# Four transformer blocks in one kernel: a length chain moved, row tests and a masked context on GpSimd, V biases folded, one norm on ScalarE and GpSimd

## The chip, the cores and the metric

The kernel runs on one core of one Trainium2 chip. The metric is the device time of one execution in microseconds (us), the lower the better. Five engines work side by side, each through its own instruction list in order, and wait for each other by semaphores: TensorE (PE), VectorE (DVE), ScalarE (ACT), GpSimd (POOL), and SyncE (SP), which only issues DMAs here.

## What is computed

32 batches of x and ctx, each 128 x 256 float32, go through four blocks with six attentions and two feed-forwards. Numbers 0 to 5 are the attentions, D = 256, 16 heads.

```python
# block L0 (attentions 0 and 1, heads of 16, no output weight)
mask0 = 1 - all(x == 0);  z = mha(x, x, Wq1, Wk1, Wv1, mask0, causal)     # attention 0
x1 = norm(x + z);         mask1 = 1 - all(x1 == 0)
z = mha(x1, ctx, Wq2, Wk2, Wv2, mask1)                                    # attention 1
x2 = norm(x1 + z)
z = (relu(x2 @ fc1.T + b1) * mask0 @ fc2.T + b2) * mask0;  x = norm(x2 + z)   # ("ff", 1)
# in mha: Q, K, V = (x|kv) @ W * mask;  energy = Q K^T
#         lengths = sum(energy[:, :, 0, :] != 0);  columns >= lengths become -inf;  softmax; @ V; * mask
# block L1: attention 2 (self, mask by row table), attention 3 (over ctx, mask by batch), then
#           gelu feed-forward 256 -> 1024 -> 256 ("ff", 3); biases on Q, K, V, output
# block L2: attention 4, heads of 64 over ctx ("wide"); block L3: attention 5 over ctx
# each attention: x = norm(x + softmax(Q K^T / sqrt(dk)) V @ Wo + bo)
```

## The kernel before

The 32 batches are worked in 4 rounds of 8 (LANES). In a round attention 0 is done for its 8 batches, then attention 1, and so on. One attention of one batch is a slot, n = 0 to 191; att(n) is its attention and batch(n) its batch. "Stage a" below is the eight slots of attention a.

`make_orders` (L125) writes each engine's order by hand: every item gets a time in slots, n plus an offset from the table NARROW or BROAD (L115 to L121), and each engine's list is sorted by it. The items of up to five slots are so interleaved. `tile(at, reader, ...)` puts an item on PE at `at` and its copy out of PSUM on `reader` at `at + AFTER_PE` (0.03). With the offsets of a narrow slot, seen from slot n's start:

- XT: transpose of X (ACT copies it out). K, Q, V: the three products, K and Q a slot early. ACT copies K; Q with a scale in four pieces into Qx (two halves of the heads), and waits for nothing else than PE. `keys`: GpSimd makes Kx of K in four operations. V goes to V16 by ACT (attentions 0, 1) or by DVE with the bias row added (2, 3, 5).
- S and T: scores of one unit (8 heads), row by row and turned. A slot has two units, u = 2n and 2n+1. One score step `ST` on PE does S of one unit and T of an earlier one in two PSUM tensors SC0 and SC1: at 0.0 S of 2n and T of 2n-3, at 0.5 S of 2n+1 and T of 2n-2. `free_scores` has PE wait until the former user of the bank is read: for an S before, until its maximum is taken; for a T before, until its exp is done. So the S of 2n+1 waits for the exp of 2n-3.
- `max` (DVE, L1084): row maxima of S, at 0.12 and 0.62. `MT` (0.86): PE turns them, DVE adds them to Qx, and the turned scores then hold score minus maximum. `exp` (ACT, L862 to L871): at 0.12 and 0.62, in a slot after.
- PV: probabilities by V, copied to OT by ACT; E1: transpose back, DVE divides by the sum; E2, E3: transpose and output weight (attentions 2, 3, 5). Attentions 0 and 1 have no output weight, and GpSimd adds the residual.
- `L` (attentions 0 and 1): the energies of row 0. GpSimd lays out q0, PE makes the product (L at n-0.42), and DVE goes through a chain: not equal, count, reciprocal, factor, row of -BIG behind the length, and two additions into Kx (seven instructions, L1046 to L1063). The S of the slot waits for it.
- `norm`: bn_stats, bn_aggr, plus eps, centre times gamma on DVE (LN); the power -0.5 on GpSimd (rstd, L1234); times rstd plus beta on DVE (LN end, L1166).
- Row tests: `seen0`, `seen1`: DVE takes the largest absolute value of each row and compares it with 0. The mask of attention 1's keys: GpSimd makes a diagonal of seen1 (`token mask`), PE multiplies ones by it (`SM`, L625), DVE multiplies the turned context CT by the result (L1015).
- Feed-forward: XF transposes X, F1 with ACT's relu or gelu, F2, DVE adds X, then a norm ("ff"). Offsets above 3 and 4 put E1 to F2 three to five slots later, so the small feed-forward (of attention 1) falls into the last four slots of stage 1 and the first four of stage 2, the large one into stage 3's last four and the wide stage.

PE's results go through four PSUM tiles in turn (M0 to M3, `free_tile`): a tile is written again when the item four back is copied out.

```python
                if before[0] == "S":
                    pe.wait_ge(maxima, done("max", before[1]))
                else:
                    pe.wait_ge(probs, done("exp", before[1]))
```

The weights, biases and rows are loaded once at the start; x, ctx and masks of later batches by SP in time.

Of the kernel before, what the change touches and what calls it, by code (L numbers as in the profile page):

```python
# [122 lines left out]


def make_orders():  # L125
# [10 lines left out]
    def norm(at, what, n):  # L136
        put("DVE", at, "LN", what, n)
        put("POOL", at + 0.01, "rstd", what, n)
        put("DVE", at + LN_END, "LN end", what, n)

    steps = {}
    for n in range(SLOTS):
# [32 lines left out]
        tile(n + o["V"], "ACT" if a in (0, 1) else "DVE", "V", n, 0)  # L175
# [62 lines left out]
def score_bank_users():  # L238
# [1076 lines left out]
```

## Time and profile before

| what | value |
|---|---|
| median of 3 runs | 2756.04 us (2753.0 to 2758.52) |
| the profiled execution | 2755.75 us, its span 2753.6 us |
| mean granted clock of TensorE | 0.952 |
| PE busy | 2519.1 us, 91% |
| DVE, ACT, POOL busy | 1600.2 (58%), 1376.2 (50%), 827.1 (30%) us |
| idle of POOL before the power of the norm | 1202.6 us in 256 |
| chain that ended last | PE 72%, DVE 11%, issue 7%, POOL 5%, ACT 4% |

The span is the time from the first to the last instruction. Busy times are of the engine's own instructions; idle time of an engine that isn't the bottleneck costs nothing. The granted clock is the share of TensorE's full 2.4 GHz; its other level is 1.2 GHz. PEld rows are weight loads, which lie beside the products.

### The profile page before, as it was taken

How to read it: one execution, taken by the hardware profiler on the slowest of the kernel's cores; microseconds unless marked ns; L12 is line 12 of the kernel's file. 1: busy time of each engine (PE TensorE's matmuls, PEld its weight loads, DVE VectorE, ACT ScalarE, POOL GpSimd, SP SyncE). 2: the span in 40 equal slices, each digit the busy share in tenths (PEclk: the TensorE clock that was granted, in tenths of full speed). 3: DMA queues.
4: the chain of work that ended last, by engine and by line, in shares of the span. 5: the costliest groups of instructions: out<-in, count | busy, mean ns of one | idle time of the engine just before them, and what ended most of it. 6: DMA issues, size and time to landing. Idle time of an engine off the chain costs nothing.

```text
span 2753.6 us, 70667 instructions
## 1 busy us (share of the span) xinstructions
PE 2519.1 (91%) x28737; PEld 2094.6 (76%) x28737; DVE 1600.2 (58%) x3528; ACT 1376.2 (50%) x3364; POOL 827.1 (30%) x1412
## 2 busy tenths in 40 slices
PE   6879999999887999999988899999998889999998
PEld 5667887887766788787766688888786668888876
DVE  4677753445766775344576676544466676644446
ACT  2344565554444456555544456555454445655544
POOL 1234322223233432222323343222232344312222
PEclk8889999999998999999999899999999889999999
DMA  7000000000100000000000000000000000000000
GB/s 245 7 2 2 2 2 1 1 1 10 36 6 2 2 2 2 1 1 2 21 26 4 2 2 2 2 1 1 1 27 23 2 2 2 2 1 1 1 1 17
DMA packets 23778, 32.28 MB, mean 12 GB/s; under 512 B 2305, under 2 KB 22177, under 8 KB 23329
## 3 DMA queue, kind: packets, MB, share of 16 engines
q1 hardware_dynamic: 23456, 27.78, 3.1%
q8 instruction: 229, 3.75, 0.6%
q14 instruction: 93, 0.75, 0.1%
HBM read 23.57 MB, written 4.19 MB: 10 GB/s over the span
## 4 chain that ended last, share of the span: by engine, by line
PE 72%; DVE 11%; issue 7%; POOL 5%; ACT 4%; POOLq 0%; DMA 0%; DVEq 0%; SPq 0%; ACTq 0%
PE M L522 40%; PE SC L685 12%; PE M L528 7%; PE M L721 4%; DVE nmax L1084 3%; POOL Kx L1202 3%; PE M L738 2%; PE SC L584 2%; PE SC L703 2%; PE SC L559 2%; ACT Pr L862 2%; DVE Kx L1063 1%; POOL Y L1228 1%; DVE stats L1151 1%; DVE len_row L1057 1%
## 5 line engine op out<-in xcount | busy, mean ns | idle before, releaser
L1234 POOL TENSOR_TENSOR rstd<-rstd,half 128x1 f32<-128x1 f32 x256 | 184.5, 721 | 1202.6 <-DVE rstd L1155 1201.7
L522 PE MATMUL M<-XT,W 128*128 128x128 f32 x4096 | 540.8, 287 | 2.5 <-ACT H L904 1.5
L522 PEld LDWEIGHTS M<-XT,W 128*128 128x128 f32 x4096 | 519.0, 203 | 20.0 <-issue 2.7
L1084 DVE TENSOR_REDUCE nmax<-SC 128x8 f32<-128x1024 f32 x320 | 389.6, 1217 | 92.0 <-PE SC L685 92.0
L1202 POOL TENSOR_SCALAR Kx<-K,own,k_ones 128x128 f32<-128x128 f32 x640 | 279.6, 451 | 498.7 <-ACT K L815 357.1
L685 PEld LDWEIGHTS SC<-Kx,Qx 32*128 32x128 f32 x5120 | 341.6, 200 | 91.9 <-issue 87.7
L685 PE MATMUL SC<-Qx,Kx 32*128 32x128 f32 x5120 | 398.4, 297 | 0.9 <-DVE Qx L1023 0.9
L685 PE MATMUL SC<-Kx,Qx 32*128 32x128 f32 x5120 | 394.7, 296 | 1.5 <-DVE nmax L1084 1.5
L685 PEld LDWEIGHTS SC<-Qx,Kx 32*128 32x128 f32 x5120 | 333.8, 198 | 3.3 <-issue 1.3
L871 ACT ACTIVATE Pr<-SC 128x1024 f32<-128x1024 f32 x256 | 261.6, 1022 | 69.7 <-PE SC L584 44.3
L841 ACT ACTIVATE Qx<-M,q_bias,q_scale 128x128 f32<-128x128 f32 x640 | 241.8, 474 | 23.4 <-PE M L522 23.4
L862 ACT ACTIVATE Pr<-SC,nmax_w 128x128 f32<-128x128 f32 x512 | 139.0, 383 | 183.3 <-DVE nmax_w L1087 158.1
L1128 DVE TENSOR_TENSOR Y<-M,X 128x256 f32<-128x256 f32 x128 | 54.1, 423 | 271.2 <-PE M L522 271.2
L522 PE MATMUL M<-CT,W 128*128 128x128 f32 x1536 | 207.5, 286 | 0.0
L522 PEld LDWEIGHTS M<-CT,W 128*128 128x128 f32 x1536 | 189.0, 197 | 14.7 <-issue 7.6
L815 ACT ACTIVATE K<-M 128x256 f32<-128x256 f32 x64 | 24.5, 383 | 336.5 <-PE M L522 336.5
L522 PE MATMUL M<-W,CT 128*128 128x512 f32 (+1 forms) x512 | 191.6, 497 | 0.0
L818 ACT ACTIVATE K<-M,CB 128x128 f32<-128x128 f32 x192 | 60.2, 366 | 260.8 <-PE M L522 260.8
L721 PE MATMUL M<-Pr,V 128*32 128x128 f32 x5120 | 173.8, 277 | 0.0
L1252 POOL TENSOR_TENSOR Pr<-Pr,wrec 128x1024 f32<-128x1024 f32 x64 | 121.3, 1895 | 156.7 <-DVE wrec L1099 156.7
L528 PE MATMUL M<-ident,nmax 128*128 128x128 f32 x160 | 48.4, 302 | 130.0 <-DVE nmax L1084 129.9
L798 ACT ACTIVATE XT<-M 128x256 f32<-128x256 f32 x256 | 97.8, 390 | 137.3 <-PE M L528 137.2
(127 smaller groups left out, 4460.3 us busy)
## 6 DMA issues: line engine op xcount, KB each, us to landing
X<-x SPq DMA_DIRECT2D x32, 128.0 KB, 2.1
c_in<-ctx_in SPq DMA_DIRECT2D x32, 128.0 KB, 2.1
out<-X SPq DMA_DIRECT2D x32, 128.0 KB, 1.7
RV<-row_vec SPq DMA_DIRECT2D x1, 2304.0 KB, 12.1
W<-w_k SPq DMA_DIRECT2D x5, 256.0 KB, 9.0
W<-w_q SPq DMA_DIRECT2D x5, 256.0 KB, 12.1
W<-w_v SPq DMA_DIRECT2D x5, 256.0 KB, 7.8
W<-w_f SPq DMA_DIRECT2D x1, 1024.0 KB, 8.9
```

The costliest lines, as they stand in the source:

```text
L522: last = pe.matmul(dst, a, b, start=(k == 0), stop=(k == len(lhsTs) - 1))
L528: last = pe.transpose(dst[:, i * P:(i + 1) * P], src[:, i * P:(i + 1) * P], ident[:, :])
L685: filled[at] = pe.matmul(dst, lhsT, rhs, start=(starting and i == 0), stop=(i == len(line) - 1), skip_group_check=True)
L721: last = pe.matmul(tile_of(it)[32 * t:32 * t + 32, b * P:(b + 1) * P], on_ring(V16, "narrow", n)[:, 4 * b + t, :], p[:, at:at + P], start= ...
L798: act.activation(XT[i % len(XT)][:, :], tile_of(it)[:, 0:D], ACT.Copy).then_inc(tile_act, 1)
L841: last = act.activation(q[:, half_of, c * P:(c + 1) * P], tile_of(it)[:, c * P:(c + 1) * P], ACT.Identity, bias=q_bias[:, which, c, half_o ...
L862: last = act.activation(p[:, i * P:(i + 1) * P], SC[u % 2][:, i * P:(i + 1) * P], ACT.Exp, bias=nm[:, i:i + 1])
L871: last = act.activation(p[:, :], SC[u % 2][:, :], ACT.Exp)
L1084: dve.tensor_reduce(nm, SC[h][:, :].rearrange("p (g c t) -> p g c t", c=KC, t=P), AX_X, ALU.max, negate=True).then_inc(maxima, 1)
L1202: last = pool.tensor_scalar(kx[:, half_of, c * P:(c + 1) * P], k[:, c * P:(c + 1) * P], own[:, half_of:half_of + 1], k_ones[:, half_of, c: ...
L1234: pool.tensor_tensor(r[:, :], r[:, :], half[:, :], ALU.pow).then_inc(rstd_done, 1)
L1252: pool.tensor_tensor(p, p, on_ring(wrec, "wide", u)[:, :].unsqueeze(2).to_broadcast([P, HU, P]), ALU.mult).then_inc(wide_norm, 1)
```

## The change

It changes offsets of the order, moves work between engines and folds constants.

- Order: on PE, L goes from n-0.42 (0.58 in a slot, behind the second score step) to n-0.64 (0.36, ahead of it). `AFTER_SCORES`, the distance of maxima and exps from their score steps, goes from 0.12 to 0.19. PV, MT, XT, K, Q, XF, F1, F2, LN get new offsets. The context's transpose goes from stage 0 to two slots ahead of its slot of attention 1.
- q0 is made from a copy of Q's first row's column by ACT (`q_col`), ahead of the four copies of Q; GpSimd does one operation on 8 columns for each half, as before.
- The length chain has six instructions in place of seven: the comparison gives -1/BIG in place of 1, the reciprocal of the count then is the value itself.
- `seen0`, `seen1`: the comparison with 0 goes to GpSimd, the largest value stays on DVE.
- The mask of attention 1: GpSimd multiplies the context itself by seen1 after PE has turned it once (`context`), PE turns it again (`CM`, two transposes), ACT copies that to CmT. Token mask, SM and DVE's product go.
- The V biases of attentions 2 to 5 no longer are added to V or to the context. Since probabilities sum to one they are multiplied by the output weight once (items VT and VB in the slots 9 to 12) and added to the rows o2 to o5. V of attention 2 is copied by ACT. The wide context is one copy in place of four with a bias.
- The norm of ("ff", 1): ACT does scale and shift (`normalise`), GpSimd multiplies by gamma and adds beta (`affine`), in place of two operations on DVE. The shift is one more small operation on GpSimd.
- Y has two buffers, mv two, absmax four.

```diff
-NARROW = dict(XT=-1.20, SM=-1.25, K=-0.92, Q=-0.86, L=-0.42, V=0.30, CT=0.40, MT=0.86, PV=2.66, E1=3.20, E2=3.54,
-              E3=3.74, XF=4.40, F1=4.62, F2={1: 4.90, 3: 5.10},
-              seen0=-1.15, keys=-0.88, q0=-0.78, mask_row=-0.30, residual=3.30, LN=3.40, SF=0.14)
+NARROW = dict(XT=-1.14, CM=-1.10, CT=-1.92, K=-0.94, Q=-0.88, L=-0.64, V=0.28, MT=0.93, PV=2.62, E1=3.20, E2=3.54,
+              E3=3.72, XF=4.24, F1=4.40, F2={1: 4.66, 3: 4.95}, seen0=-1.0, context=-1.75, keys=-0.80, q0=-0.86,
+              mask_row=-0.30, residual=3.32, LN=3.84)
+V_BIAS_AT = {2: 9.32, 3: 10.32, 4: 11.32, 5: 12.32}
-AFTER_PE, AFTER_SCORES = 0.03, 0.12
-LN_END = 0.25
+AFTER_PE, AFTER_SCORES = 0.03, 0.19
+LN_END = 0.22
+def by_pool(norm):
+    return norm[0] == "ff" and att(norm[1]) == 1
...
     def norm(at, what, n):
         put("DVE", at, "LN", what, n)
         put("POOL", at + 0.01, "rstd", what, n)
-        put("DVE", at + LN_END, "LN end", what, n)
+        if by_pool((what, n)):
+            put("ACT", at + 0.12, "normalise", what, n)
+            put("POOL", at + 0.18, "affine", what, n)
+        else:
+            put("DVE", at + LN_END, "LN end", what, n)
...
-            put("DVE", n + o["seen0"], "seen0", b)
+            put("DVE", n + o["seen0"], "largest0", b)
+            put("POOL", n + o["seen0"] + 0.08, "seen0", b)
+        if a == 1:
             tile(n + o["CT"], "ACT", "CT", b)
-        if a == 1:
-            put("POOL", n + o["SM"] - 0.20, "token mask", n)
-            tile(n + o["SM"], "DVE", "SM", n)
+            put("POOL", n + o["context"], "context", b)
+            tile(n + o["CM"], "ACT", "CM", b)
...
-        tile(n + o["V"], "ACT" if a in (0, 1) else "DVE", "V", n, 0)
+        tile(n + o["V"], "ACT" if a in (0, 1, 2) else "DVE", "V", n, 0)
...
-        put("SP", slot(b, 0) - 1.5 if b >= 2 else -9, "c", b)
+        put("SP", slot(b, 1) - 3 if b >= 2 else -9, "c", b)
...
-                    sp.wait_ge(tile_full, done("tile", ("CT", b - 2)))
+                    sp.wait_ge(tile_full, done("tile", ("CM", b - 2)))
...
+                elif kind == "CM":
+                    b = it[1]
+                    pe.wait_ge(cm_done, done("batch", b))
+                    turn(tile_of(it), c_in[b % 2], KC).then_inc(tile_full, 1)
+                elif kind == "VB":
+                    a = it[1]
+                    if a == WIDE:
+                        pe.wait_ge(v_bias_wide, 1)
+                        by_tokens(it, "o4", split(Qw, 4) + split(Kw, 4), D)
+                    else:
+                        evicted(("VT", a))
+                        by_tokens(it, f"o{a}", split(Qw, KC), D)
...
+                elif kind == "normalise":
+                    key = it[1:]
+                    i = AT["affine"][key]
+                    act.wait_ge(mean_done, i + 1)
...
+                    act.activation(xn[i % 2], on_ring(Y, "norm", key)[:, :], ACT.Identity, bias=shift[i % 2][:, 0:1],
+                                   scale=rstd[j][:, 0:1]).then_inc(normalised, 1)
...
+                        act.activation(q_col[i % 2][:, :], chunks(tile_of(it)[:, 0:D])[:, :, 0], ACT.Copy,
+                                       scale=DK ** -0.5).then_inc(q_first, 1)
...
-                    dve.reciprocal(crec[:, :], cnt[:, :]).then_inc(len_rec, 1)
-                    dve.wait_ge(len_rec, done("length", n))
-                    dve.scalar_tensor_tensor(out=lval[:, :], in0=crec[:, :], scalar=-BIG, in1=cnt[:, :], op0=ALU.mult,
-                                             op1=ALU.mult).then_inc(len_val, 1)
+                    dve.reciprocal(lval[:, :], cnt[:, :]).then_inc(len_val, 1)
...
+                    pool.tensor_scalar(c_in[b % 2][:, :], c_in[b % 2][:, :], seen1[lane(b)][:, 0:1], None,
+                                       ALU.mult).then_inc(cm_done, 1)
...
+                        pool.tensor_scalar(shift[i % 2][:, :], mv[AT["norm"][key] % 2][:, 0:1], r[:, 0:1], -1.0, ALU.mult,
+                                           ALU.mult).then_inc(mean_done, 1)
+                elif kind == "affine":
...
+                    pool.tensor_tensor(xn[i % 2], xn[i % 2], row(name + "g"), ALU.mult).then_inc(affine_half, 1)
+                    pool.wait_ge(affine_half, i + 1)
+                    pool.tensor_tensor(X[lane(b)][:, :], xn[i % 2], row(name + "b"), ALU.add).then_inc(normed_pool, 1)
```

## Rows read from the trace of the kernel before

**Rows 1.** The page: the span, and busy time of each engine.

```profile
span 2753.6 us, 70667 instructions
PE 2519.1 (91%) x28737; PEld 2094.6 (76%) x28737; DVE 1600.2 (58%) x3528; ACT 1376.2 (50%) x3364; POOL 827.1 (30%) x1412
```

**Rows 2.** Stretches of attentions 0 to 5: length, PE, PEld, DVE, ACT, POOL, PEclk, DMA.

```profile
713.30:813.00 99.70, 83.79 (x1101) 65.55 (x1100) 67.13 (x171) 41.59 (x89) 28.71 (x66) 0.93 0.05 16
813.00:919.30 106.30, 86.77 (x1092) 73.18 (x1093) 74.57 (x177) 45.09 (x98) 42.45 (x83) 0.86 0.01 2
919.30:1001.70 82.40, 82.40 (x1146) 65.65 (x1148) 57.52 (x124) 42.76 (x95) 32.41 (x59) 1.00 0.01 2
1001.70:1098.60 96.90, 96.02 (x1196) 84.27 (x1189) 58.16 (x131) 59.94 (x129) 26.93 (x47) 1.00 0.01 2
1098.60:1314.30 215.70, 204.89 (x1654) 172.16 (x1652) 91.55 (x170) 114.93 (x348) 52.90 (x51) 0.98 0.01 1
1314.30:1389.30 75.00, 71.10 (x1012) 59.31 (x1012) 49.58 (x106) 39.05 (x84) 23.38 (x48) 0.98 0.08 25
```

**Rows 3.** Waits: who for whom; us in all, times, longest us.

```profile
PE M L528 <- DVE nmax L1084: 129.9, 71, 3.5
...
PE M L625 <- POOL seen_diag L1219: 30.0, 32, 1.5
...
PE M L738 <- ACT Pr L878: 16.4, 12, 2.1
```

**Rows 4.** Timeline, PE, stage 2: start us, length us, instructions.

```profile
974.17 1.95 PE L522 MATMUL M<-XT,W 128*128 128x128 f32 x16
...
977.26 0.59 PE L559 MATMUL SC<-mask_ss_b,ident_b 128*128 128x512 bf16 x2
...
979.34 0.38 PE L528 MATMUL M<-ident,O 128*128 128x128 f32 x2
...
979.65 1.08 PE L721 MATMUL M<-Pr,V 128*32 128x128 f32 x32
...
981.95 0.59 PE L559 MATMUL SC<-mask_ss_b,ident_b 128*128 128x512 bf16 x2
```

**Rows 5.** Timeline, ACT, the same slot.

```profile
975.27 0.62 ACT L818 ACTIVATE K<-M,CB 128x128 f32<-128x128 f32 x2 [2.69 <-PE M L522]
...
975.78 1.02 ACT L871 ACTIVATE Pr<-SC 128x1024 f32<-128x1024 f32 x1
...
976.68 1.51 ACT L841 ACTIVATE Qx<-M,q_bias,q_scale 128x128 f32<-128x128 f32 x4
...
980.94 0.61 ACT L885 ACTIVATE OT<-M 128x512 f32<-128x512 f32 x1
```

**Rows 6.** Timeline, PE, a slot of stage 0; in brackets the idle time before.

```profile
773.14 0.44 PE L528 MATMUL M<-ident,X 128*128 128x128 f32 x2
775.94 0.39 PE L528 MATMUL M<-ident,nmax 128*128 128x128 f32 x1 [2.35 <-DVE nmax L1084]
```

**Rows 7.** Timeline, DVE, a feed-forward slot of stage 1.

```profile
870.75 0.47 DVE L1137 SCALAR_TENSOR_TENSOR Y<-M,seen,X 128x256 f32<-128x256 f32 x1
...
871.25 0.43 DVE L1151 BATCH_NORM_STATS2 stats<-Y 128x6 f32<-128x256 f32 x1
...
871.92 0.15 DVE L1155 TENSOR_SCALAR rstd<-mv 128x1 f32<-128x1 f32 x1
...
872.39 1.22 DVE L1084 TENSOR_REDUCE nmax<-SC 128x8 f32<-128x1024 f32 x1
```

**Rows 8.** Groups by line and form: busy us, mean ns; idle before, releaser.

```profile
L1234 POOL TENSOR_TENSOR rstd<-rstd,half 128x1 f32<-128x1 f32 x256 | 184.5, 721 | 1202.6 <-DVE rstd L1155 1201.7
...
L1245 POOL TENSOR_TENSOR X<-X,RV 128x256 f32<-128x256 f32 x160 | 117.0, 736 | 22.2 <-PE M L528 22.1
...
L798 ACT ACTIVATE XT<-M 128x256 f32<-128x256 f32 x256 | 97.8, 390 | 137.3 <-PE M L528 137.2
...
L522 PE MATMUL M<-W,OT 128*128 128x256 f32 x512 | 116.2, 380 | 0.7 <-ACT OT L889 0.7
```

More of the change, by code:

```diff
@@ L197, in make_orders @@
         if a == 0:
-            put("DVE", n + o["LN"] + LN_END + 0.01, "seen1", b)
+            put("DVE", n + o["LN"] + LN_END + 0.02, "largest1", b)
+            put("POOL", n + o["LN"] + LN_END + 0.08, "seen1", b)
         if a in XT_FOR_FF:
@@ L208, in make_orders @@
         put("PE", at, "ST", parts.get("S"), parts.get("T"))
+    for a, at in V_BIAS_AT.items():
+        if a == WIDE:
+            put("DVE", at, "v bias wide", a)
+        else:
+            tile(at, "DVE", "VT", a)
+        tile(at + 0.40, "DVE", "VB", a)
     for b in range(BATCH):
@@ L271 @@
     "norm_end": [it[1:] for it in pick("DVE", {"LN end"})],
+    "affine": [it[1:] for it in pick("POOL", {"affine"})],
     "add": [it[1:] for it in pick("POOL", {"add"})],
@@ L279 @@
 BANK_BEFORE = score_bank_users()
-assert INDEX["norm"] == INDEX["rstd"] == INDEX["norm_end"] and INDEX["length"] == INDEX["q0"]
+assert INDEX["norm"] == INDEX["rstd"] and INDEX["norm_end"] == [key for key in INDEX["norm"] if not by_pool(key)]
+assert INDEX["affine"] == [it[1:] for it in pick("ACT", {"normalise"})] and INDEX["length"] == INDEX["q0"]
 assert INDEX["narrow"] == INDEX["keys"] == INDEX["e1"]
@@ L389, in build @@
             sem("len_done"))
+        v_bias_wide = sem("v_bias_wide")
         recip_done, summed = sem("recip_done"), sem("summed")
@@ L486, in _ @@
                 elif kind == "store":
-                    sp.wait_ge(normed, done("norm", ("att", slot(b, 5))))
+                    sp.wait_ge(normed, done("norm_end", ("att", slot(b, 5))))
                     sp.dma_start(out[b, :, :], X[lane(b)][:, :]).then_inc(stored[lane(b)], 16)
@@ L613, in _ @@
                         what, a = XT_AFTER[j]
-                        pe.wait_ge(normed, done("norm", (what, slot(b, a))))
+                        if by_pool((what, slot(b, a))):
+                            pe.wait_ge(normed_pool, done("affine", (what, slot(b, a))))
+                        else:
+                            pe.wait_ge(normed, done("norm_end", (what, slot(b, a))))
                     turn(tile_of(it), X[lane(b)], KC).then_inc(tile_full, 1)
@@ L883, in _ @@
                         act.wait_ge(tile_full, done("tile", ("E1", before[1]) if before[0] == "PV" else ("E3", before[1] // 2)))
-                    if kind == "PV":
-                        last = act.activation(o[:, :], tile_of(it)[:, :], ACT.Copy)
-                    else:
-                        for t in range(4):
-                            last = act.activation(o[:, t * P:(t + 1) * P], tile_of(it)[:, t * P:(t + 1) * P],
-                                                  ACT.Identity, bias=bias("v4", 4 * (it[1] % 2) + t))
-                    last.then_inc(tile_act, 1)
+                    act.activation(o[:, :], tile_of(it)[:, :], ACT.Copy).then_inc(tile_act, 1)
                 elif kind == "E2":
@@ L900, in _ @@
                     a, i = att(n), AT["ff"][n]
+                    if a == 3:
+                        once(normed_pool, LANES * (batch(n) // LANES + 1))
                     if i:
@@ L967, in _, with free_sum @@
             dve.wait_ge(masks_turned, 1)
+            dve.tensor_scalar(iota[:, :], iota[:, :], -1.0 / BIG, None, ALU.mult)
             dve.tensor_copy(key_bias[:, :], M[TILES - 1][:, 0:BATCH]).then_inc(ready_dve, 1)
+            def free_sum(key):
+                i = AT["norm"][key]
+                if i >= len(Y):
+                    before = INDEX["norm"][i - len(Y)]
+                    if by_pool(before):
+                        once(normalised, done("affine", before))
+                    else:
+                        once(centred, done("norm_end", before))
             for it in ORDER["DVE"]:
@@ L1125, in _ @@
                     dve.wait_ge(added, done("add", (XT_FOR_ATT[att(n)], batch(n))))
-                    if AT["norm"][("att", n)]:
-                        once(centred, AT["norm"][("att", n)])
+                    free_sum(("att", n))
                     dve.tensor_tensor(on_ring(Y, "norm", ("att", n))[:, :], tile_of(it)[:, 0:D],
@@ L1133, in _ @@
                     dve.wait_ge(added, done("add", (XT_FOR_FF[a], b)))
-                    once(centred, AT["norm"][("ff", n)])
+                    free_sum(("ff", n))
                     y = on_ring(Y, "norm", ("ff", n))
@@ L1226, in _ @@
                     if i >= len(Y):
-                        pool.wait_ge(centred, i - len(Y) + 1)
+                        before = INDEX["norm"][i - len(Y)]
+                        if by_pool(before):
+                            pool.wait_ge(normalised, done("affine", before))
+                        else:
+                            pool.wait_ge(centred, done("norm_end", before))
                     pool.tensor_tensor(on_ring(Y, "norm", key)[:, :], on_ring(O, "e1", n)[:, :], X[lane(b)][:, :],
@@ L1239, in _ @@
                     once(rows_in if name == "g0" else rows_late_in, 16)
+                    if name[0] == "o":
+                        once(tile_dve, done("tile_dve", ("VB", int(name[1]))))
                     if name == "g0":
```

153 lines of the change are left out of this document (95 added, 58 removed).

## The prediction, made before the changed kernel was run

> **What bounds the kernel now.** First the page's busy line: PE 2519.1 of 2753.6 us (91%), no other engine above 58% [rows 1]. Then the table of stretches over one of the four rounds (8 batches, 48 slots, 676 us): 99.7 us for the eight slots of attention 0, 106.3 for attention 1, then 82.4, 96.9, 215.7 (the wide one) and 75.0 [rows 2]. In stages 2 and 3 PE is busy without a hole and its granted clock is 1.00, the level of 2.4 GHz. In stages 0 and 1 it is busy for 84 and 87 us only, and the clock is 0.93 and 0.86, so part of the time passes at 1.2 GHz. The waits say why: PE's transpose of the row maxima (MT) waits 129.9 us in all for `nmax` on DVE, and the token-mask product 30.0 us for `seen_diag` [rows 3]. In a slot of stage 0 the first is one hole of 2.35 us behind the transpose of X [rows 6]: on DVE the second maximum stands behind the length chain. So stages 2, 3 and most of 5 are bound by PE's own stream and can only lose by a new wait; stages 0 and 1 are bound by waits and can win.
>
> **ScalarE's order is turned round.** A slot has two score steps, ST0 and ST1. ST1 writes into the bank in which ST0's turned scores stand, so (free_scores) it waits for their exp; the next slot's ST0 waits in the same way for the exp of ST1's. With AFTER_SCORES at 0.19 for 0.12, Q at n+0.15 and K at n+0.09, the first exp, so far between K and Q, stands behind Q. PV goes from 0.69 to 0.65, so the second exp (0.62, now 0.69) stands behind the context copy. ScalarE takes its queue in order: an exp whose scores are ready still waits for the product ahead of it. That ACT is idle half of the span does not help, since it idles while PE makes Q.
> Price in stage 2. K and Q run on PE from 974.17 to 976.12, ST1 starts 977.26, PV 979.65, the next ST0 981.95 [rows 4]. ACT has exp from 975.78 (1.02), then Q (four in 1.51) [rows 5]. After: Q 976.15 to 977.66, exp right behind with 0.1 of overlap to 978.58, ST1 at 978.61, which is 1.35 later. PV then ends on PE at 979.65 + 1.35 + 1.08 = 982.08, its copy (0.61 [rows 5]) at 982.72, the second exp at 983.64; the next ST0, due at 983.30, starts 983.67, 0.37 more. Together 1.72 a slot. It holds where PE has only E1 and V between Q and ST1: the last four slots of stage 2, the first four of stage 3, the last five of stage 5, 13 x 1.72 = 22.4. The slot before these in stage 5 has less on PE and loses some 2.7 by the same walk.
> In four slots of stage 3 the product F1 now stands ahead of ST1 and needs the copy of XT, which stands behind the exp. With K's start as 0: Q's copies end 3.5, exp 4.42, XT's copy 4.75, F1 starts 4.8 where PE is free at 3.4: 1.4 x 4 = 5.6.
>
> **Eight slots with the small feed-forward (four of stage 1, four of stage 2).** F2 now stands at 0.66 on PE and its sum at 0.69 on DVE, put ahead of the second maximum (also 0.69); `normalise` stands on ACT at 0.83, ahead of XT, CM and the next K, and nothing on ACT passes it. Walk in stage 2: F1 starts 4.8 as above (1.4 late), ST1 5.7, PV 7.8, F2 8.7 to 9.7; on DVE the sum 0.47 and the maximum 1.22, to 11.36 [rows 7]; only then MT (1.4 late), ST0, and K at 13.6. The other branch from the maximum: bn_stats to eps 0.82, with the hand-over 0.91 [rows 7], the power on GpSimd 0.72 [rows 8], the shift (128x1, not in this trace; between 0 and that power's 0.72, I take 0.2 since it has no power), normalise and XT's copy 0.39 each [rows 8]: K at 13.95. Before: a later slot is 974.17 to 981.95 plus the 2.08 of a score step [rows 4], 9.86, which leaves 82.4 - 39.4 = 43.0 for the first four. After 55.7 (four of 13.95, less one shorter ST, plus one E2): +12.7. In stage 1 CM and CT come on top and one slot has no length chain: 14.0, 14.0, 13.6, 13.1 = 54.7.
>
> **Where the length chain goes.** In the other slots of stages 0 and 1 L stands on PE ahead of ST1, and on DVE between the maxima, so MT's 2.35 us go. (q0 is now made from a first copy of two columns of Q; it costs ACT between 0 and the 0.38 of a whole 128 columns, I take 0.25, as it has hardly anything to read.) What is late next is again the exp. Stage 0: Q on PE ends 1.95, ACT is through at 4.6, ST1 at 4.63, PV ends 3.16 later, its copy and the exp 4.72 later, ST0 at 9.38, K at 11.46: 8 x 11.46 = 91.7 at the full clock, with two waits of 1.1 and 1.35 in place of the one. Stage 1, first four: CT moves Q's end to 2.18, ST1 4.85, ST0 8.6, K 9.65; with 1.1 for two longer score steps 39.7, and with the last four 94.4. Before, the clock cost these stages (1 - 0.93) x 99.7 = 7.0 and (1 - 0.86) x 106.3 = 14.9 [rows 2]. Waits stay in every slot, so I put 5.3 and 9 back, and 3 in the first half of stage 2; the bounds are 0 and the costs of before.
>
> **The other parts.** CM's two transposes (0.38, as E2's two in rows 4) take the place of the mask product inside the walks above. DVE loses the product with the mask, two passes of one norm, V's row sum and one link of the chain; PE waits for DVE in the places of [rows 3] alone, so elsewhere this is worth nothing. GpSimd gains `context` (256 columns: up to the 0.74 of its two-input sum) and the affine, 2 x 0.74 [rows 8]; it is idle 70% [rows 1], and the affine ends 1.1 us after the next K starts, before `keys` has its input. PVW as one copy in place of four: PE waited 16.4 us in all for the copies beside it [rows 3], so 0 to -4.1 a round, I take -2. Folding the V biases once in round 0: the wide one as an E3 of the wide attention, 116.2/32 = 3.6 us [rows 8], three narrow ones a quarter of it each, 2.7, and three turned rows 1.1, all on PE: 7 us once. SP reloads c_in behind CM, three slots ahead of its use, some 30 us: hidden.
>
> **Sum of a round.** Stage 0: 97.0 - 99.7 = -2.7. Stage 1: 94.4 + 9 - 106.3 = -2.9. Stage 2: 12.7 + 3 + 6.9 = +22.6. Stage 3: 6.9 + 5.6 = +12.5. Stage 4: -2. Stage 5: 5 x 1.6 (its ST is shorter) + 2.7 = +10.7. That is +38.2, 153 in four rounds, 160 with the 7: on the profiled execution's own 2755.75 (its span and 2.15 around it), which is 0.3 below the median 2756.04, 2916 us.
>
> **Rivals.**
> A. The clock spreads. Waits of 1.3 us now stand in stages 2, 3 and 5. For: the stages with a wait in every slot are those at 0.93 and 0.86. Against: that was one of 2.35. If the 254 us of these stages fall to 0.93 they lose 18 more a round: 2916 + 72 = 2988. The Trainium skill ("TensorE: Matmul & The Clock Gate", section "A second HAM failure mode: psum-queue depth-cycling") says that frequent short idling between groups of matmuls makes the clock swing between its two levels; no row here shows whether waits of 1.3 us do.
> B. Faster: VectorE's relief is worth all it can be. The waits for maxima and mask (160 us [rows 3]) and the clock of stages 0 and 1 (4 x 21.9 = 88) come back whole, because DVE and not ACT sets the pace there: 2756 - 248 + 7 + 170 (the losses of stages 2, 3 and 5 at full clock) = 2685. It is faster than before once over 177 of the 248 are won. For: the largest wait on the page is its target. Against: in the walk the exp ends later than the maximum in each of these slots.
> C. F2, maximum and normalise overlap more than in my walk, and no clock is lost: 2916 - 4 x 17.3 - 4 x 7 (half of what those slots lose or fail to win) = 2819.
> D. Gains and losses cancel within 0.2%, about what a measurement here can tell from nothing.
>
> **Numbers.** Forecast 0.64, A 0.12, B 0.11, C 0.10, D 0.03. The forecast's own range is 2847 (no clock lost, 20.9 x 4 + 7) to 2960; with most of A and C it is 2825 to 2990. Faster 0.11, same 0.03, slower 0.86.
>
> **What would show it.** In the changed trace PE waits at the score steps for ACT Pr, about 1.3 us in most narrow slots and over 100 us in all; the wait for nmax is gone from stage 0 and stands in the eight feed-forward slots, about 1.4 each; stage 2 is near 105 us and stage 5 near 86. I am wrong if PE shows no waits for the exp, or if stages 2, 3 and 5 keep 82.4, 96.9 and 75.0.

## The result, and the profile after

The changed kernel takes 2831.39 us (median of 4 runs, 2828.23 to 2832.09) where the one before takes 2757.28 (2753.0 to 2758.53): 1.0269 times, 95% interval 1.0252 to 1.0287. The direction is the forecast's and the size is half of it: 76 us between the profiled executions (2832.09 against 2755.75), where 160 were forecast. The time lies below the forecast's own range (2847 to 2960). The late slots along ScalarE's queue came out as the walks had them; what was put too high was the cost of TensorE's clock and the time of the wide stage.

The page after, beside [rows 1]: PE is busy 40 us less and the span is 77 us longer.

```profile
span 2830.2 us, 70971 instructions
PE 2479.0 (88%) x28803; PEld 2033.3 (72%) x28803; DVE 1547.6 (55%) x3282; ACT 1384.2 (49%) x3332; POOL 926.0 (33%) x1572
```

The same round by stretches, in the columns of [rows 2] (length, PE, PEld, DVE, ACT, POOL, PEclk, DMA share, GB/s):

```profile
715.00:807.00 92.00, 79.31 (x1101) 59.85 (x1101) 68.47 (x156) 41.39 (x95) 33.39 (x75) 1.00 0.06 17
807.00:906.00 99.00, 79.43 (x1098) 68.22 (x1099) 66.41 (x143) 48.59 (x116) 48.55 (x92) 0.93 0.03 9
906.00:1012.30 106.30, 86.28 (x1129) 64.61 (x1128) 50.83 (x114) 49.32 (x111) 44.84 (x79) 1.00 0.01 2
1012.30:1124.20 111.90, 100.80 (x1284) 86.73 (x1284) 60.22 (x136) 62.88 (x130) 29.72 (x52) 1.00 0.01 2
1124.20:1328.60 204.40, 199.26 (x1649) 167.64 (x1648) 93.91 (x176) 104.60 (x299) 50.42 (x47) 1.00 0.01 1
1328.60:1414.40 85.80, 72.87 (x937) 60.87 (x936) 44.80 (x87) 38.64 (x84) 24.49 (x48) 0.92 0.05 14
```

| stage of round 1 | before | forecast | after | clock before, after |
|---|---|---|---|---|
| 0 | 99.7 | 97.0 | 92.0 | 0.95, 1.00 |
| 1 | 106.3 | 103.4 | 99.0 | 0.84, 0.93 |
| 2 | 82.4 | 105.0 | 106.3 | 1.00, 1.00 |
| 3 | 96.9 | 109.4 | 111.9 | 1.00, 1.00 |
| 4 (wide) | 215.7 | 213.7 | 204.4 | 0.98, 1.00 |
| 5 | 75.0 | 85.7 | 85.8 | 0.95, 0.92 |
| sum | 676.0 | 714.2 | 699.4 | |

The clocks before are not those of [rows 2]. Its stretches start 9.8 us behind the first score step of each stage: the first step with the causal mask in this round starts at 703.52, where the rows begin at 713.30. The lengths hold to 0.1 us, but busy times and clocks are of the shifted stretches. In the right place stages 0, 1 and 5 read

```profile
703.50:803.10 99.60, 84.05 (x1111) 65.58 (x1110) 68.43 (x176) 42.45 (x91) 27.90 (x64) 0.95 0.07 20
803.10:909.50 106.40, 86.51 (x1081) 72.90 (x1081) 71.75 (x173) 43.69 (x93) 40.27 (x81) 0.84 0.01 2
1304.50:1379.50 75.00, 69.19 (x937) 58.26 (x936) 44.32 (x88) 39.41 (x89) 24.33 (x47) 0.95 0.07 20
```

The loss is in stages 2 and 3 (+38.9) and in stage 5 (+10.8); the other three gained 26.3. PE's waits after, whole span (who for whom; us in all, times, longest), against [rows 3]:

```profile
PE M L546 <- ACT XT L835: 70.4, 67, 1.6
PE SC L722 <- ACT Pr L929: 69.2, 92, 1.6
PE SC L583 <- ACT Pr L929: 68.8, 87, 1.2
PE M L552 <- DVE nmax L1143: 59.1, 52, 1.6
...
PE SC L722 <- ACT Pr L927: 14.4, 20, 1.3
PE M L546 <- ACT CmT L845: 12.4, 7, 1.8
```

The score steps wait for an exp (L927, L929) 152 us in all, and did not before. The wait for the maxima fell from 129.9 to 59.1, the one for the mask is gone, and a new one of 70.4 for ScalarE's copy of XT stands at K and F1. A late slot of stage 2 on PE shows the first two, beside [rows 4]:

```profile
979.46 1.95 PE L546 MATMUL M<-XT,W 128*128 128x128 f32 x16
...
981.68 1.03 PE L546 MATMUL M<-W,XT 128*128 128x256 f32 x4
983.91 0.60 PE L583 MATMUL SC<-mask_ss_b,ident_b 128*128 128x512 bf16 x2 [1.21 <-ACT Pr L929]
```

and ScalarE in the same slot, beside [rows 5]:

```profile
980.55 0.62 ACT L869 ACTIVATE K<-M,CB 128x128 f32<-128x128 f32 x2 [2.95 <-PE M L546]
981.44 1.50 ACT L899 ACTIVATE Qx<-M,q_bias,q_scale 128x128 f32<-128x128 f32 x4 [0.27 <-PE M L546]
982.83 1.03 ACT L929 ACTIVATE Pr<-SC 128x1024 f32<-128x1024 f32 x1
```

K is copied, then ScalarE goes straight on to Q, and the exp, whose scores had long been ready, begins only at 982.83. PE has nothing left at 982.70 and stands for 1.21 us. The late slots of stage 2 are 11.7 us long (9.9 before): +1.8, where the walk gave 1.72.

A slot with the small feed-forward, first on PE, then on DVE, GpSimd and ScalarE:

```profile
908.83 2.02 PE L546 MATMUL M<-XT,W 128*128 128x128 f32 x16 [1.13 <-ACT XT L835]
...
913.73 1.13 PE L546 MATMUL M<-XT,W 128*128 128x128 f32 x8 [1.35 <-ACT XT L835]
...
920.17 0.33 PE L552 MATMUL M<-ident,nmax 128*128 128x128 f32 x1 [1.49 <-DVE nmax L1143]
```
```profile
918.50 0.48 DVE L1195 SCALAR_TENSOR_TENSOR Y<-M,seen,X 128x256 f32<-128x256 f32 x1 [6.39 <-PE M L546]
918.90 1.22 DVE L1143 TENSOR_REDUCE nmax<-SC 128x8 f32<-128x1024 f32 x1
```
```profile
920.93 0.55 POOL L1314 TENSOR_TENSOR rstd<-rstd,half 128x1 f32<-128x1 f32 x1 [6.20 <-DVE rstd L1220]
921.58 0.53 POOL L1321 TENSOR_SCALAR shift<-mv,rstd 128x1 f32<-128x1 f32 x1
```
```profile
922.15 0.60 ACT L853 ACTIVATE H<-Y,shift,rstd 128x256 f32<-128x256 f32 x1 [3.17 <-POOL shift L1321]
922.66 0.36 ACT L835 ACTIVATE XT<-M 128x256 f32<-128x256 f32 x1
```

The second maximum starts 0.40 after the feed-forward's sum, which waited 6.39 us for F2, and ends at 920.12: MT waits 1.49 (forecast 1.4). ScalarE's queue stands 3.17 us at `normalise`; the copy of XT behind it needs nothing of it (PE had turned that X at 918.30, before `normalise` began). Such slots of stage 2 last 14.3, 14.9, 14.9 and 15.2 us; the walk gave 13.95. In stage 1 they last 12.6, 16.4, 15.9 and 13.8 (walk: 14.0, 14.0, 13.6, 13.1).

### The profile page after: what moved, and what is told of

It reads as the page before. It is cut to its first block, busy times and chain, and to the rows that moved or that the text cites. A ratio compares the mean times of both kernels' runs of the same rounds, so it can differ in the third digit from the quotient of the medians.

```text
span 2830.2 us, 70971 instructions
## 1 busy us (share of the span) xinstructions
PE 2479.0 (88%) x28803; PEld 2033.3 (72%) x28803; DVE 1547.6 (55%) x3282; ACT 1384.2 (49%) x3332; POOL 926.0 (33%) x1572
## 4 chain that ended last, share of the span: by engine, by line
PE 62%; ACT 14%; issue 12%; POOL 8%; DVE 3%; ACTq 0%; POOLq 0%; DMA 0%; SPq 0%; DVEq 0%
PE M L546 34%; PE SC L722 10%; ACT Pr L929 6%; PE M L552 5%; ACT Qx L899 4%; PE M L758 4%; PE M L775 2%; PE SC L740 2%; PE SC L608 2%; POOL Kx L1268 2%; PE SC L583 2%; ACT Pr L927 1%; POOL X L1343 1%; ACT Pr L920 1%; POOL H L1328 1%
## 5 line engine op out<-in xcount | busy, mean ns | idle before, releaser
L546 PE MATMUL M<-XT,W 128*128 128x128 f32 x4096 | 528.4, 281 | 70.4 <-ACT XT L835 70.4
L1314 POOL TENSOR_TENSOR rstd<-rstd,half 128x1 f32<-128x1 f32 x256 | 174.6, 682 | 1260.6 <-DVE rstd L1220 1260.6
L546 PEld LDWEIGHTS M<-XT,W 128*128 128x128 f32 x4096 | 499.0, 196 | 99.9 <-ACT XT L835 83.3
L722 PEld LDWEIGHTS SC<-Kx,Qx 32*128 32x128 f32 x5120 | 319.4, 188 | 141.9 <-ACT Pr L929 77.3
L722 PE MATMUL SC<-Kx,Qx 32*128 32x128 f32 x5120 | 369.1, 283 | 58.5 <-ACT Pr L929 57.6
L722 PE MATMUL SC<-Qx,Kx 32*128 32x128 f32 x5120 | 371.2, 283 | 0.9 <-DVE Qx L1089 0.9
L722 PEld LDWEIGHTS SC<-Qx,Kx 32*128 32x128 f32 x5120 | 310.3, 186 | 3.1 <-ACT Pr L929 1.1
L942 ACT ACTIVATE OT<-M 128x512 f32<-128x512 f32 x224 | 134.3, 599 | 315.6 <-PE M L758 215.7
L929 ACT ACTIVATE Pr<-SC 128x1024 f32<-128x1024 f32 x256 | 263.2, 1028 | 9.2 <-PE SC L722 7.2
L546 PEld LDWEIGHTS M<-CT,W 128*128 128x128 f32 x1536 | 187.6, 196 | 14.9 <-issue 6.7
L758 PEld LDWEIGHTS M<-Pr,V 128*32 128x32 f32 x5120 | 130.0, 109 | 33.2 <-issue 27.9
L546 PE MATMUL M<-W,H 128*128 128x256 f32 x640 | 152.0, 384 | 0.0
## 6 DMA issues: line engine op xcount, KB each, us to landing
W<-w_q SPq DMA_DIRECT2D x5, 256.0 KB, 12.4
```

Source lines behind the costliest of these rows:

```text
L546: last = pe.matmul(dst, a, b, start=(k == 0), stop=(k == len(lhsTs) - 1))
L722: filled[at] = pe.matmul(dst, lhsT, rhs, start=(starting and i == 0), stop=(i == len(line) - 1), skip_group_check=True)
L758: last = pe.matmul(tile_of(it)[32 * t:32 * t + 32, b * P:(b + 1) * P], on_ring(V16, "narrow", n)[:, 4 * b + t, :], p[:, at:at + P], start= ...
L929: last = act.activation(p[:, :], SC[u % 2][:, :], ACT.Exp)
L942: act.activation(o[:, :], tile_of(it)[:, :], ACT.Copy).then_inc(tile_act, 1)
L1314: pool.tensor_tensor(r[:, :], r[:, :], half[:, :], ALU.pow).then_inc(rstd_done, 1)
```

## The experiments

Theory T, in all of them: the loss is ScalarE's order, exps and maxima put behind work that waits for PE (AFTER_SCORES 0.19), with the wait at `normalise`; the length chain's new place is a gain on its own. Its rival R: the maxima on DVE, or the new operations themselves (context, affine, copies of CM), set the pace. Each kernel was timed beside the kernel before; ratios are to that, with the 95% interval.

**The exps alone back.**

```diff
-            put("ACT", n + T_STEP[h] + AFTER_SCORES, "exp", u)
+            put("ACT", n + T_STEP[h] + 0.12, "exp", u)
```

> The changed kernel with the exps alone put back to 0.12 and 0.62 (maxima stay at 0.19 and 0.69). Theory 1 (the exp behind Q and behind the context copy is what PE waits for in the score steps): the waits of PE at score steps for ACT Pr, 36.6 us a round in the changed kernel's trace, go; a slot of stage 0 falls from 11.5 to about 9.5, a late slot of stage 2 from 11.7 to 9.9, of stage 5 from 9.8 to 8.3; feed-forward slots keep their wait for the maximum. About 35 to 45 us a round less: 2831 -> 2650 to 2690. Rival (the exp only looks late because VectorE or the feed-forward chain sets the pace, and the wait moves on): less than 40 us in all, 2790 or more. Rival 2 (a tighter stream loses the full clock again): waits go but the mean clock falls below 0.96, 2720 to 2760.

Measured 2695.6 us, 0.9771 (0.9746 to 0.9796): 136 us less than the changed kernel, by one number, and 6 above the expected range. The waits of the score steps for the exp are gone, and stages 2 and 5 are 97.7 and 75.8.

**The maxima alone back.**

```diff
-            put("DVE", n + S_STEP[h] + AFTER_SCORES, "max", u)
+            put("DVE", n + S_STEP[h] + 0.12, "max", u)
```

> The changed kernel with the maxima alone put back to 0.12 and 0.62 (exps stay at 0.19 and 0.69), so the second maximum comes before F2's sum on VectorE. Theory 1: PE's waits at MT in the eight small feed-forward slots (14 us a round) go, but K still waits for normalise and XT behind it on ScalarE, so a slot falls from 14.9 to about 13.3: 10 to 13 us a round, 2831 -> 2780 to 2790. Rival (normalise sets the whole of these slots): the same within 10 us. Rival 2 (waits only add up): the full 14 and more, below 2775.

Measured 2792.31, 1.0128 (1.0111 to 1.0145): 39 us less, 2 above the expected range. It is stages 1 and 2, the slots with the feed-forward (99.0 to 92.6, 106.3 to 102.6), where the waits for nmax fall from 59.1 to 16.3 us in all; the exp waits stay. Maxima and exps are two separate costs of one number.

**Both back.**

```diff
-AFTER_PE, AFTER_SCORES = 0.03, 0.19
+AFTER_PE, AFTER_SCORES = 0.03, 0.12
```

> The changed kernel with AFTER_SCORES back at 0.12, all other parts of the change kept. Theory 1: both gains add, 2600 to 2650, well under the kernel before (2757), because the moved length chain is worth what it was meant for once the exp is in time. Rival (the change loses by its other parts, the norm on ScalarE and GpSimd and the extra transposes): 2757 or more.

Measured 2661.68, 0.9661 (0.9645 to 0.9677), a little above the expected range: the parts give 136 + 39 = 175, both together 170. So all the rest of the change makes the kernel 3.4% faster. ScalarE in a late slot of stage 2, to be held against the one above:

```profile
921.95 0.62 ACT L869 ACTIVATE K<-M,CB 128x128 f32<-128x128 f32 x2 [2.69 <-PE M L546]
922.46 1.02 ACT L929 ACTIVATE Pr<-SC 128x1024 f32<-128x1024 f32 x1
923.36 1.51 ACT L899 ACTIVATE Qx<-M,q_bias,q_scale 128x128 f32<-128x128 f32 x4
```

The exp fills the time in which ScalarE would have waited for Q. The largest wait that remains is 64.1 us for XT's copy, which stands behind `normalise`; the norm's own experiments are below.

**The late order in the kernel before.** The same number alone, on the other side.

```diff
-AFTER_PE, AFTER_SCORES = 0.03, 0.12
+AFTER_PE, AFTER_SCORES = 0.03, 0.19
```

> The kernel before with AFTER_SCORES 0.19 alone. Theory 1: 1.35 to 1.7 us in each narrow slot of stages 2, 3 and 5, and in stages 0 and 1 the later score step also moves the length chain: 40 to 58 us a round, 2920 to 2990. Rival (harmless by itself, only with K and Q earlier does it turn the order): Q stands at 0.17 in that kernel, so 0.19 turns it as well; if the time stays within 20 us of 2757 the exp is not what PE waits for.

Measured 3009.92, 1.0922 (1.0906 to 1.0939), again above the range: +252 here, against 170 in the changed kernel. Its waits and its stage 0 show why:

```profile
PE M L528 <- DVE nmax L1084: 179.0, 71, 3.5
PE SC L685 <- ACT Pr L871: 82.4, 91, 1.6
PE SC L559 <- ACT Pr L871: 72.6, 90, 1.4
PE SC L685 <- ACT Pr L869: 49.3, 44, 2.0
```
```profile
764.70:885.60 120.90, 92.06 (x1111) 70.32 (x1110) 70.36 (x179) 42.23 (x91) 27.87 (x64) 0.88 0.06 17
```

With the chain at its old place the late maximum lengthens MT's wait as well, 129.9 to 179.0 us, and the clock of stage 0 goes to 0.88. The waits for the exp are also longer here, 204.3 us in these three rows against 152.4 in the changed kernel. The cost of a late order depends on what it adds to.

**The chain's place, from both sides.** In the changed kernel, L alone back:

```diff
-NARROW = dict(XT=-1.14, CM=-1.10, CT=-1.92, K=-0.94, Q=-0.88, L=-0.64, ...
+NARROW = dict(XT=-1.14, CM=-1.10, CT=-1.92, K=-0.94, Q=-0.88, L=-0.42, ...
```

> The changed kernel with L alone back at n-0.42: behind the second score step on PE, ahead of the second maximum on VectorE. Theory (the move is worth the 2.35 us wait of MT in each slot with a length chain, and the clock that this long wait costs): stage 0 back above 100 us with its clock near 0.9, stage 1 above 105: 20 to 30 us a round more, 2831 -> 2910 to 2950. Rival (the exp sets these slots, so the place of L is worth nothing here): within 20 us of 2831. Of the clock: if the length of a single wait decides it, not their sum, the clock falls in stage 0 in this run, where PE has one wait of over 2 us again, and stays at 1.00 in stage 2, whose waits sum to 23 us in the changed kernel too.

Measured 2953.7, 1.0706 (1.0683 to 1.0729): 122 us more than the changed kernel and just above the expected range: without the chain's new place the change would have lost 195. MT waits again, 14.9 us in stage 0 and 15.3 in stage 1:

```profile
746.50:853.20 106.70, 82.83 (x1101) 62.40 (x1101) 63.97 (x152) 41.70 (x95) 32.76 (x74) 0.97 0.05 16
853.20:965.10 111.90, 82.84 (x1099) 70.36 (x1099) 61.53 (x147) 48.45 (x114) 49.34 (x93) 0.92 0.02 6
```

I had expected a clock near 0.9 in stage 0; it is 0.97. And in the kernel before, the offsets that belong to the chain's place (K, Q, L, `keys`, q0, the residual, LN and its end):

```diff
-NARROW = dict(XT=-1.20, SM=-1.25, K=-0.92, Q=-0.86, L=-0.42, ...
+NARROW = dict(XT=-1.20, SM=-1.25, K=-0.94, Q=-0.88, L=-0.64, ...
-              seen0=-1.15, keys=-0.88, q0=-0.78, mask_row=-0.30, residual=3.30, LN=3.40, SF=0.14)
+              seen0=-1.15, keys=-0.80, q0=-0.82, mask_row=-0.30, residual=3.32, LN=3.84, SF=0.14)
-LN_END = 0.25
+LN_END = 0.22
```

> The kernel before with the length chain's part of the order alone: K -0.94, Q -0.88, L -0.64, keys -0.80, q0 -0.82, residual 3.32, LN 3.84 and its end 0.22; AFTER_SCORES stays 0.12, nothing moves between engines. Theory 1 (the place of L ahead of the second maximum is what makes stages 0 and 1 fast, and no moved work is needed for it): MT's waits of 30 us a round mostly go, and the clock of stages 0 and 1 returns to over 0.97: 30 to 45 us a round, 2757 -> 2580 to 2640. Rival (without the early copy q_col the product L waits for Q's four copies, and without GpSimd's help VectorE is short): 2690 or more.

Measured 2656.67, 0.9642 (0.9627 to 0.9656): 100 us faster than before, by offsets alone, yet short of the expected 2580 to 2640. LN moved too (3.40 to 3.84) and was not tried by itself, so only the run above is of L alone. Its first waits suggest what the early copy of two columns of Q (q_col) is for:

```profile
PE M L522 <- POOL q L1189: 68.9, 62, 2.1
PE M L528 <- DVE nmax L1084: 51.7, 56, 1.6
```

Without that copy q0 comes from the last of Q's four copies, and the earlier L waits for it, about 1.1 us in 62 slots. In the changed kernel PE waits for q once, for 1.0 us. No run has q_col as its only difference.

**The norm on ScalarE and GpSimd, with the exps and maxima back.** First taken away (the eight normalisations a round go back to VectorE):

```diff
-    return norm[0] == "ff" and att(norm[1]) == 1
+    return False
...
-                    if a == 3:
-                        once(normed_pool, LANES * (batch(n) // LANES + 1))
```

> Built on e3 (AFTER_SCORES 0.12, the rest of the change kept): the norm of the small feed-forward goes back to VectorE whole, no normalise on ScalarE and no affine on GpSimd. Theory 1 (PE's waits of K and XT in the eight feed-forward slots, 7.3 us each in stages 1 and 2 of a round, come from normalise standing ahead of XT, CM and K on ScalarE): they go, 8 to 14 us a round, 2662 -> 2605 to 2630. Rival (VectorE is short in these slots, so its two operations come back as a wait for the maxima): 2650 or more, with the wait of MT for nmax up by as much.

Measured 2596.04, 0.941 (0.939 to 0.943): 66 us less than with it, more than expected; the waits for XT's copy fall from 64.1 to 22.8 us. Then kept, but later in the two queues:

```diff
-            put("ACT", at + 0.12, "normalise", what, n)
-            put("POOL", at + 0.18, "affine", what, n)
+            put("ACT", at + 0.30, "normalise", what, n)
+            put("POOL", at + 0.36, "affine", what, n)
```

> Built on e3: normalise stays on ScalarE and the affine on GpSimd, but both 0.18 of a slot later, behind XT and CM. Theory 1: as in e5 the waits of K go, and VectorE stays relieved: 2600 to 2625, at or below e5. Rival (what delays K is the time of the whole norm, or GpSimd, not the place in ScalarE's queue): as e3 within 10 us.

Measured 2605.11, 0.9446 (0.9423 to 0.9469): 57 of the 66 us come back by place alone; the 9 that are left are above the expected "at or below" the run with the norm on VectorE. The waits for XT's copy are 32.8 us here. So the work cost little, and its place ahead of XT, CM and K most. That it is the place in ScalarE's queue is what these waits say; GpSimd's part was moved in the same run, and the two were not separated.

**Four copies of the wide PV again, in the changed kernel.**

```diff
-                    act.activation(o[:, :], tile_of(it)[:, :], ACT.Copy).then_inc(tile_act, 1)
+                    if kind == "PV":
+                        last = act.activation(o[:, :], tile_of(it)[:, :], ACT.Copy)
+                    else:
+                        for t in range(4):
+                            last = act.activation(o[:, t * P:(t + 1) * P], tile_of(it)[:, t * P:(t + 1) * P], ACT.Copy)
+                    last.then_inc(tile_act, 1)
```

> The changed kernel with the wide context copied in four pieces again (without a bias, same output). The wide stage fell from 215.7 to 204.4 us where -2 was forecast. Theory 1 (the moved feed-forward and the clock made that, the one copy little): 0 to 4 us a round, 2831 -> 2831 to 2847. Rival (the single copy shortens the chain TP, PVW, E3 that PE waits for): 5 to 9 us a round, 2851 to 2867.

Measured 2826.51, 1.0251 (1.0223 to 1.0278), stage 4 still 204.4. The single copy is worth nothing: with four the time is 5 us lower, just outside the expected range, and the interval overlaps that of the changed kernel.

**The feed-forward's place, in the changed kernel.**

```diff
-              E3=3.72, XF=4.24, F1=4.40, F2={1: 4.66, 3: 4.95}, ...
+              E3=3.72, XF=4.40, F1=4.62, F2={1: 4.90, 3: 5.10}, ...
```

> The changed kernel with the feed-forward's offsets back (XF 4.40, F1 4.62, F2 4.90 and 5.10), so F1 stands behind the second score step and F2 behind MT. Asks where the unforeseen gain of the wide stage (215.7 -> 204.4) came from. Theory 1 (one F2 of 3.6 us falls in stage 3 instead of the wide stage, and the shorter waits keep its clock full): the wide stage returns to 209 to 216 us, stage 3 falls by 5 to 8 us (its F2 moves out, its waits of F1 for XT's copy go), the two together 4 to 6 less than the 316 of the changed kernel; the eight small feed-forward slots lose the MT wait and the F1 wait, 2 us each: 2831 -> 2740 to 2790 in all. Rival (the moved feed-forward is what made the wide stage short): stages 3 and 4 together rise, 2831 or more.

Measured 2794.21, 1.0136 (1.012 to 1.0151). The time came within the range and its parts did not all: stages 1 and 2 are 23 shorter, but stages 3 and 4 together rise from 316.3 to 328.4 where 4 to 6 less was expected.

```profile
987.20:1108.20 121.00, 101.81 (x1269) 88.06 (x1269) 60.72 (x135) 62.47 (x130) 29.09 (x52) 0.96 0.01 2
1108.20:1315.60 207.40, 203.52 (x1665) 171.37 (x1665) 94.52 (x178) 105.38 (x299) 49.86 (x47) 1.00 0.01 1
```

With F1 behind ST1 nothing stands between Q and that score step, and the wait for the late exp is in the open: the waits for L927 are 57.9 us in all here, against 14.4. In the changed kernel F1 covered them.

**A version out of this.** Exps and maxima back, the norm on VectorE, and F1 just behind ST1 (F1=4.53 for 4.40), so that it no longer waits for XT's copy:

> Built on e5 (AFTER_SCORES 0.12, norm on VectorE): F1 at 4.53, behind the second score step on PE instead of ahead of it. Theory 1 (PE's waits of F1 for XT's copy, 3.1 us in stage 2 and 3.7 in stage 3 of a round, come from F1 standing too close behind XT): they go, 5 to 8 us a round, 2596 -> 2565 to 2580. Rival (F2 then waits for F1's copy out, the wait only moves): 2590 to 2610.

Measured 2575.49, 0.935 (0.9335 to 0.9366), the fastest of all and within the expected range; its clock is 0.993. Stages 0 and 3 take 82.0 and 104.3 us, stages 1 and 2:

```profile
738.50:821.80 83.30, 74.82 (x1099) 62.76 (x1099) 70.03 (x152) 45.50 (x112) 44.25 (x84) 1.00 0.04 10
821.80:905.80 84.00, 83.24 (x1130) 65.78 (x1128) 54.96 (x124) 45.33 (x105) 37.27 (x64) 1.00 0.01 2
```

On top of it, the large feed-forward's F2 later (F2 at 5.08 for 4.95):

> Built on e10: F2 of the large feed-forward at 5.08 (between K and Q of the next slot) for 4.95. Theory (its 3.8 us a round of waiting for F1's copies by gelu lies in the three slots where F2 follows MT at once; K in front of it covers them): 2 to 4 us a round, 2575 -> 2560 to 2568. Rival (ScalarE's two gelu passes and the exps are the bound of those slots, so the wait moves to Q or to the score step): within 5 us of 2575.

Measured 2580.03, 0.9354 (0.9339 to 0.937), no gain: F2's waits went (14.0 us in all, 3.5 a round; the profile puts them down to the copy OT, not to gelu as I had it), and 4.8 a round at the score steps came (4.0 for the late exp, 0.8 for a copy of DVE), as the rival had it.

## Why the forecast was right in direction and wrong in size

**The order on ScalarE: right.** 1.72 a slot was forecast for the late slots of stage 2 and 1.8 measured; stage 5 came to 85.8 for 85.7 (83.4 in two other rounds). The exps alone, put back, give 136 us; the cause is shown.

**The chain's place: right.** In stage 0 the walk gave 11.46 a slot and measured are 11.5; the 2.35 us hole of [rows 6] is gone, and in its place PE waits 12.9 us for the exp, in 17 pieces of 1.2 at most. The first four slots of stage 1 were put at 9.65 and are 10.6, 10.1, 9.8 and 9.8. The chain alone, put back, costs 122 us.

**The feed-forward slots: right in form, short by 0.4 to 1.3 a slot in stage 2.** The groups of the three operations that the trace before did not show say where:

```profile
L853 ACT ACTIVATE H<-Y,shift,rstd 128x256 f32<-128x256 f32 x32 | 19.2, 599 | 100.1 <-POOL shift L1321 100.1
L1321 POOL TENSOR_SCALAR shift<-mv,rstd 128x1 f32<-128x1 f32 x32 | 15.5, 485 | 3.3
L895 ACT ACTIVATE q_col<-M 128x2 f32<-128x2 f32 x64 | 11.0, 172 | 36.7 <-PE M L546 36.7
```

I took 0.2 for the shift because it has no power: 0.485. I took the 0.39 of a copy for `normalise`: 0.60. Both stand on the path to XT's copy and give 0.5 of the miss of a slot. Without its clock term the walk gave 102.0 for stage 2, and 106.3 were measured at the full clock: that the sum of 105.0 lies near is luck, 3 too much of clock against 4.3 too little of walk. The q_col copy, taken at 0.25, is 0.17. The idle time of L853, 100.1 us over 32, is ScalarE's 3.1 us at each `normalise`.

**The clock: the first step that failed.** "Waits stay in every slot, so I put 5.3 and 9 back, and 3 in the first half of stage 2." Those are 17.3 us a round. Stage 0 took 92.0 us where the walk alone had 91.7, and its clock was 1.00. Stage 2 stayed at 1.00. Stage 1 stood at 0.93, and what that costs can be read from the run with four copies, in which stage 1 has one order and nearly the same waits (21.1 and 20.2 us) in rounds 1 and 2, once at the full clock and once below it:

```profile
807.70:903.10 95.40, 74.75 (x1099) 62.79 (x1100) 67.15 (x143) 48.55 (x116) 48.72 (x92) 1.00 0.03 9
1503.70:1602.80 99.10, 79.51 (x1099) 68.24 (x1100) 66.49 (x143) 48.74 (x116) 48.76 (x92) 0.93 0.03 8
```

It costs 3.7 us. So 13.6 of the 17.3 were too much, 54 in four rounds, of an error of 85. The pair also shows that one minus the granted clock, times the length, is not the price: that product is 6.9 here. My 7.0 and 14.9 were such products, and for the shifted stretches at that (with the clocks 0.95 and 0.84 they are 5.0 and 17.0, so their sum hardly moves).

The clock came back elsewhere too. Stage 4's 3.4, which I had left in, went. The first stage of round 0, the row before and then the row after, is where the most came back that I had not counted:

```profile
20.40:129.90 109.50, 88.76 (x968) 69.77 (x968) 58.80 (x144) 37.67 (x83) 25.07 (x60) 0.84 0.31 108
```
```profile
19.20:110.80 91.60, 76.95 (x960) 57.62 (x960) 58.51 (x125) 36.29 (x86) 30.48 (x71) 0.95 0.35 125
```

It is 17.9 us shorter, where I had let every round gain 2.7. By the product 12.9 of it are clock (0.16 x 109.5 = 17.5 against 0.05 x 91.6 = 4.6), which by the pair above is an upper bound. Over the whole span the product fell from 132 to 49 us, where my terms left some 114.

The range failed with these terms. Its lower end, 2847, has them all at nothing and still lies 15 us above the time, so the clock in stages 0 to 2 is not the whole error. Its upper end, 2960, is not worked out: the costs of before in stages 0 and 1 give 2916 + 4 x 7.6 = 2946.

Rival A, the clock spreading, did not hold: stage 2 has 21.3 us of PE waits after (for XT, nmax and exp) and none before, and stays at 1.00, and so does stage 3 with 11.3; stage 5 goes from 0.95 to 0.92, and in the next round not at all (0.96). The Trainium skill ("TensorE: Matmul & The Clock Gate", section "A second HAM failure mode: psum-queue depth-cycling") tells of frequent short idling that makes the clock swing; in stages 2 and 3 the trace does not agree. Rival C lies nearest by its number, 2819, but only its half on the clock came true; the slots with F2, maximum and normalise were longer than in my walk, not shorter.

What decides the clock here stays open. By the waits inside each stage 0: after, 12.9 us in pieces up to 1.2, clock 1.00; before, 15.6 us up to 2.4, 0.95; with the chain put back, 25.1 us up to 2.1, 0.97; with the late order in the kernel before, 30.2 us up to 3.4, 0.88. In these four the clock follows the longest single wait rather than the sum. But stage 5 after has 12.9 us in pieces up to 1.6 and 0.92, where stage 2 has 21.3 up to 1.5 and 1.00, and the pair above has the same waits at two clocks. So the waits of a stage alone do not settle it, and no run changed the length of a wait at a fixed sum.

**The wide stage: the second step that failed, a hole overlooked.** "PVW as one copy in place of four [...] I take -2"; measured were -11.3, and none of it by that copy (204.4 us with four copies as well). The trace before has this, on PE and then on ScalarE:

```profile
1114.68 1.12 PE L528 MATMUL M<-ident,Pr 128*128 128x128 f32 x4 [4.75 <-ACT H L904]
```
```profile
1110.01 2.17 ACT L862 ACTIVATE Pr<-SC,nmax_w 128x128 f32<-128x128 f32 x8 [6.23 <-PE M L721]
1112.20 1.28 ACT L904 ACT_TABLE_LOAD   x1
1113.49 2.17 ACT L904 ACTIVATE H<-M,CB 128x128 f32<-128x128 f32 x8
```

Eight gelus and the load of their table stood behind a wide exp, while PE waited for the tile, once a round. After, the F1 of that slot is ahead and the hole is absent. It is also absent with the late order alone in the kernel before (stage 4 at 208.4), and with the late order taken out of the changed kernel (203.3). So the late order is enough to take it away, and so is the rest of the change; which part of the rest was not tried, but the chain's offsets are not enough (it stands there still, 4.7 us once a round). These 4.75, at most 3.4 of clock, and an F2 of 3.6 us that moved into stage 3 (whose +15.0 had been put at +12.5) make 11.75 where 11.3 were measured. Both stages together: +10.5 forecast, +3.7 measured, 27 us over four rounds. With the 54 of the clock terms and the 10 by which the first stage gained more in round 0 than in round 1, less some 21 for walks that ran short in stages 1 and 2, that leaves 15 of the 85 us without a name.

**The parts expected to be hidden.** No wait of PE names the masked context, the reload of c_in or the tiles of the V biases. CM's copy on ScalarE does appear (CmT, 12.4 us in all), but as a victim: with the norm back on VectorE it is 1.1.

## What to carry to other kernels

In a queue worked in order, place an operation by when its own input is ready. An exp that is ready must stand ahead of a copy that still waits for a product; seven hundredths of a slot cost 170 us here, with ScalarE idle half of the time, and hid a change worth 95. The same holds for a new piece of work: the norm moved to ScalarE and GpSimd cost 57 of its 66 us by its place, not its length. Keep the clock apart from the walk's terms, with nothing lost as one end of its range, and price it from two stretches of the same work at both levels: the granted clock's shortfall times the length was nearly twice the cost here (6.9 for 3.7). Before that, list every hole of PE above 1 us in the trace before, since one per round that no edit names can still go.

## What was not expected of the hardware

A GpSimd operation on one column has no single price: a comparison with 0 (tensor_scalar, 128x1) takes 226 ns in one row test and 291 in the other, and `shift`, the same operation with a second operand and two multiplications, 485, behind a power of 682. What makes the difference was not tried. ScalarE needs 599 ns for 128x256 from SBUF with bias and scale by column, against 390 for the plain copy from PSUM [rows 8], and 172 for 128x2. Changes of the activation table cost 1.28 us each (the ACT_TABLE_LOAD row above) and can fall into the middle of a queue that PE waits for.

One link of the length chain on VectorE has several prices in the changed kernel:

```profile
L1116 DVE TENSOR_SCALAR len_row<-iota,cnt,lval 128x128 f32<-128x128 f32 x64 | 39.8, 622 | 2.3
```

It takes 345 to 348 ns in the 16 slots in which GpSimd does nothing beside it, 689 to 711 in 12 in which it runs beside one GpSimd sum of two tensors (Y<-O,X), and 1.17 to 1.55 us in 8 in which it also runs beside a product of two tensors (g_seen<-RV,seen). In the kernel before, 52 of the 64 ran with GpSimd idle and took 345 to 349. That the GpSimd operations are the cause is read from what ran side by side; no run moved one of them alone.
